# Scores and turned scores of one image in four PSUM banks, with maximum and exponential in two halves each: an audio encoder block on one Trainium2 core

## The reference

```python
# 1. time-delay layer with batch norm: windows of 5 frames, 115 values
y = relu(patches @ W.T + b)                       # (32, 121, 128)
h = (y - mean(y)) * rsqrt(var(y) + 1e-5) * gamma + beta
# 2. attention, per image, 8 heads of 16, bias per key column and head
z = layernorm(h)
scores = q(z) @ k(z).T / 4 + col_bias             # (32, 8, 121, 121)
h = h + o_proj(softmax(scores) @ v(z))
# 3. top-1 mixture of 8 experts, 128 -> 512 -> 128
z = layernorm(h)
e, gate = argmax(z @ Wr + br), 1                  # a softmax over one value is 1
h = h + relu(z @ W1[e] + b1[e]) @ W2[e] + b2[e]
```

## Time and profile before

| | us |
|---|---|
| median of three runs | 311.4 (311.34 to 316.01) |
| the profiled execution | 310.43 |
| its span in the trace | 308.7 |
| attention loop, maximum of image 0 to the last turned maximum | 45.3 to 199.0 |
| first matmul of the expert stage's first tile | 224.6 |

### The profile page before, as it was taken

One profiled execution on the slowest core, in us unless ns is written; L12 is line 12 of the kernel. 1 busy time (PEld: TensorE's weight loads), 2 busy tenths in 40 slices (PEclk: granted clock), 3 DMA queues, 4 the chain that ended last, 5 costly groups with the idle time before them and its releaser, 6 DMA issues.

```text
span 308.7 us, 9094 instructions
## 1 busy us (share of the span) xinstructions
PE 263.8 (85%) x2915; PEld 223.6 (72%) x2915; DVE 187.5 (61%) x690; ACT 165.3 (54%) x395; POOL 141.8 (46%) x256
## 2 busy tenths in 40 slices
PE   3898479999999999999999999883099999999960
PEld 2767357778778777877778786562099999999960
DVE  3887233476777768677686777746436556555540
ACT  3861122566655666466664654521067777777730
POOL 7000640343438646476565654347215555555560
PEclk9995575999999999999999999955579999999996
DMA  3200399100001101010010110111243334334200
GB/s 104 71 2 0 98 345 317 47 3 2 2 3 35 32 18 35 19 37 25 28 32 19 34 35 18 35 52 49 74 115 86 101 87 120 98 93 122 79 7 0
DMA packets 15374, 19.14 MB, mean 62 GB/s; under 512 B 4007, under 2 KB 11467, under 8 KB 15328
## 3 DMA queue, kind: packets, MB, share of 16 engines
q1 hardware_dynamic: 11888, 12.15, 14.0%
q0 software_dynamic: 3296, 6.00, 6.6%
q10 hardware_dynamic: 144, 0.41, 0.4%
HBM read 10.58 MB, written 8.47 MB: 62 GB/s over the span
## 4 chain that ended last, share of the span: by engine, by line
PE 71%; issue 9%; POOL 7%; DVE 5%; ACT 3%; DMA 2%; SPq 1%; POOLq 0%; DVEq 0%
PE psS L1089 11%; PE psS L921 10%; PE psB L904 9%; PE psO L1052 5%; PE psO L1100 5%; PE psU L1100 5%; PE psU L1001 4%; PE psU L1005 4%; PE psB L893 3%; POOL region_d L376 3%; PE psB L910 2%; DVE nmax L750 2%; ACT patT L421 2%; PE psU L1044 2%; PE psS L928 2%
## 5 line engine op out<-in xcount | busy, mean ns | idle before, releaser
L404 POOL DMA_INDIRECT out<-y_out,sidx x38 | 36.9, 971 | 45.6 <-DVE y_out L824 41.2
L495 ACT ACTIVATE PT<-psS 121x968 f32<-121x968 f32 x32 | 31.3, 977 | 37.7 <-PE psS L928 37.7
L921 PE MATMUL psS<-kT,qT 32*121 32x121 f32 x512 | 45.7, 294 | 4.9 <-ACT xT L448 2.0
L376 POOL DMA_INDIRECT region_d<-rows,pos x32 | 34.7, 1085 | 31.2 <-DVE pos L709 21.2
L928 PE MATMUL psS<-qm,kT 32*121 32x121 f32 x512 | 45.7, 295 | 0.0
L833 DVE TENSOR_SCALAR hT<-psS,b1T 128x128 f32<-128x128 f32 x76 | 23.3, 347 | 34.9 <-PE psS L1089 34.8
L921 PEld LDWEIGHTS psS<-kT,qT 32*121 32x121 f32 x512 | 34.1, 185 | 13.7 <-issue 9.3
L1089 PE MATMUL psS<-xgT,W_tile 128*128 128x128 f32 x304 | 41.7, 282 | 0.0
L750 DVE TENSOR_REDUCE nmax<-psS 121x8 f32<-121x968 f32 x32 | 37.0, 1157 | 5.6 <-PE psS L921 5.5
L1089 PEld LDWEIGHTS psS<-xgT,W_tile 128*128 128x128 f32 x304 | 38.5, 199 | 0.0
L928 PEld LDWEIGHTS psS<-qm,kT 32*121 32x121 f32 x512 | 33.6, 185 | 0.4 <-DVE qm L765 0.3
(11 more groups left out here) (222 smaller groups left out, 578.4 us busy)
## 6 DMA issues: line engine op xcount, KB each, us to landing
xg<-region_d SPq DMA_DIRECT2D x38, 129.0 KB, 2.1
W_sb<-in_L_ffn_W SPq DMA_DIRECT2D x1, 2048.0 KB, 9.9
region_d<-pads SPq DMA_DIRECT2D x1, 1032.0 KB, 6.9
region_d<-pads SPq DMA_DIRECT2D x1, 903.0 KB, 8.8
out<-y_out,sidx POOLq DMA_INDIRECT x38, 2.8
b_bc<-in_L_ffn_b SPq DMA_DIRECT2D x1, 512.0 KB, 5.1
region_d<-rows,pos POOLq DMA_INDIRECT x32, 3.0
xs<-in_x ACTq DMA_DIRECT2D x1, 402.5 KB, 3.6
```

The lines of the kernel that those rows point to most:

```text
L376: pool.indirect_dma_start(region_d, bass.IndirectOffsetOnAxis(pos[0:L, b:b + 1], 0), rows[0:L, b, E:E + ROW], None, bounds_check=E * CAP - ...
L404: pool.indirect_dma_start(out, bass.IndirectOffsetOnAxis(sidx[:, s:s + 1], 0), y_out[:, u, :], None, bounds_check=N - 1, oob_is_err=False) ...
L495: act.activation(PT[0:L, (t - 1) % 2, :, :, :], score_set(t - 1), ACT.Exp).then_inc(s_exp, 1)
L921: ins = pe.matmul(psJ[0:L, t % 2 * HG + j, a * 128:a * 128 + L], qT[rws, t // 2 % 2, a, n0:n0 + L], kT[rws, t // 2 % 2, a, n0:n0 + L], sta ...
```

## The change

It rearranges the attention loop. Scores of image t take the first half of the columns of all four banks, the turned scores of image t - 1 the second half. `scores` and `scores_T` are now one block each, without the wait for the first half (`s_half`). DVE takes the maximum of banks 0 and 1, then that of banks 2 and 3; ACT takes the exponential of banks 2 and 3, then that of banks 0 and 1; each waits for the other before it crosses over. What follows the product with V comes one step later than before for each image (`has(t, 3)` to `has(t, 5)` in place of 2 to 4), the denominators are turned back with two whole transposes, `on` is scaled in two instructions, and the ranks move from `psU` to the second bank of `psB`. The order within each engine's step is new. `h0_copy(p + 3)` stands at the end of the even step, `squares1(p + 2)` near the end of DVE's even step. POOL's order is as it was, but for `rstd2`, of image t - 4 now. The bodies of `h0_copy`, `norm1_first`, `norm1_second`, `squares1`, `k_copy`, `q_copy` and the expert functions are unchanged.

```diff
-            return b0 + nb + 4
+            return b0 + nb + 5
...
-        psJ = psS[:, :, :].rearrange("p b (h n) -> p (b h) n", n=256)
-        def score_set(t):
-            return psJ[0:L, t % 2 * HG:t % 2 * HG + HG, :].rearrange("p j (a n) -> p j a n", a=2)[:, :, :, 0:L]
+        def score_half(turned, pair):
+            return psS[0:L, 2 * pair:2 * pair + 2, turned * 256:turned * 256 + 256].rearrange("p j (a n) -> p j a n", a=2)[:, :, :, 0:L]
...
@@ POOL
-                if has(t, 3):
-                    rstd2(t - 3)
+                if has(t, 4):
+                    rstd2(t - 4)
...
@@ ACT
             for t in range(STEPS):
                 p, even = t // 2, t % 2 == 0
-                if has(t, 2):
-                    act.wait_ge(s_PV, t - 1)
-                    act.activation(OTs[:, :, :], ...
-                if not even and p + 3 < NP:
-                    h0_copy(p + 3, psB[:, 1, :])
+                if not even and p + 1 < NP:
+                    q_copy(p + 1, psB[:, 0, :])
                 if even and p > 0 and p + 3 < NP:
                     batch_norm(p + 3)
-                if has(t, 4):
-                    b = t - 4
+                if has(t, 5):
+                    b = t - 5
                     act.wait_ge(s_r2, b + 1)
                     act.activation(rows[0:L, b, WX:WX + D], rows[0:L, b, E:E + D], ACT.Identity,
                                    scale=rs2[0:L, b % 4:b % 4 + 1]).then_inc(s_x2, 1)
                 if has(t, 1):
                     act.wait_ge(s_ST, t)
+                    if has(t, 0):
+                        act.wait_ge(s_S, t + 1)
                     if t >= 3:
                         act.wait_ge(s_PV, t - 2)
-                    act.activation(PT[0:L, (t - 1) % 2, :, :, :], score_set(t - 1), ACT.Exp).then_inc(s_exp, 1)
+                    act.activation(PT[0:L, (t - 1) % 2, 2:4, :, :], score_half(1, 1), ACT.Exp).then_inc(s_exp, 1)
+                if has(t, 4):
+                    act.wait_ge(s_OT, t - 3)
+                    act.activation(oT[:, :], psO[:, 256:256 + L], ACT.Identity).then_inc(s_oT, 1)
+                if has(t, 1):
+                    if has(t, 0):
+                        act.wait_ge(s_max, 2 * t + 1)
+                    act.activation(PT[0:L, (t - 1) % 2, 0:2, :, :], score_half(1, 0), ACT.Exp).then_inc(s_exp, 1)
+                if even and p < NP:
+                    v_copy(p, psB[:, 0, :])
                 if has(t, 2):
+                    act.wait_ge(s_PV, t - 1)
+                    act.activation(OTs[:, :, :], ...
+                if even and p + 3 < NP:
+                    h0_copy(p + 3, psB[:, 1, :])
                 if not even and p + 2 < NP:
                     xT_copy(p + 2, psB[:, 1, :])
...
@@ DVE
-                if not even and p + 1 < NP:
-                    k_copy(p + 1)
-                if even and p >= 1 and p + 2 < NP:
-                    squares1(p + 2)
...
+                if has(t, 0):
+                    dve.wait_ge(s_S, t + 1)
+                    if t > 0:
+                        dve.wait_ge(s_ST, t)
+                    for pair in range(2):
+                        if pair == 1 and t > 0:
+                            dve.wait_ge(s_exp, 2 * t - 1)
+                        dve.tensor_reduce(..., score_half(0, pair), AX.X, ALU.max, negate=True).then_inc(s_max, 1)
+                for g in range(NG):
+                    if ranked(g) == t:
+                        row_places(g)
+                if has(t, 5):
+                    ... (lg of image t - 5)
+                if has(t, 0):
+                    dve.wait_ge(s_nT, t + 1)
+                    dve.tensor_tensor(qm[:, :, :], ...
+                if not even and p + 1 < NP:
+                    k_copy(p + 1)
+                if has(t, 4):
+                    dve.wait_ge(s_P, t - 3)
                 if has(t, 3):
+                    ... (rden, then on in two instructions)
+                if has(t, 4):
+                    ... (rows, then sq2, of image t - 4)
+                if even and p >= 1 and p + 2 < NP:
+                    squares1(p + 2)
+                for g in range(NG):
+                    if ranked(g) - 1 == t:
+                        expert_max(g)
+                        expert_rank(g)
+                        expert_onehot(g)
+                        expert_seen(g)
...
@@ PE, the order of a step after; waits in brackets
+ scores(t)        [exponential of t - 2, maximum of t - 1; even: k_copy and q_copy of the pair]
+ scores_T(t - 1)  [qm of t - 1]
+ turn on(t - 4)   [on; OTs(t - 3)]
+ turn back t - 3  [rows of t - 5; OTs(t - 3)], two transposes into psU
+ even: values(p), transpose_h0(p + 3); odd: k projection of p + 1 [q_copy of p + 1]
+ output projection of t - 4 [oT]
+ rank_rows if due (odd steps)
+ turn nmax(t)     [both maxima], the mark
+ product with V of t - 2
+ even: q projection of p + 1 [v_copy]; odd: transpose_xn(p + 2)
```

More of the change, by code:

```diff
@@ L988, in _ @@
                         pe.wait_ge(s_qs, 2 * p + 2)
+                    scores(t)
                 if has(t, 1):
                     pe.wait_ge(s_qm, t)
-                if t <= B:
-                    scores(t, 0)
-                if has(t, 3):
-                    if t >= 4:
-                        pe.wait_ge(s_h1, t - 3)
-                    for g in range(NG):
-                        if ranked(g) + 2 == t:
-                            pe.wait_ge(r_pick, g + 1)
-                    pe.wait_ge(s_oT, t - 2)
-                    pe.matmul(psU[0:L, 128:128 + WX], oT[:, :], owX[:, :], start=True, stop=True).then_inc(s_P, 1)
-                if has(t, 2):
-                    pe.wait_ge(s_OTs, t - 1)
+                    scores_T(t - 1)
+                if has(t, 4):
+                    pe.wait_ge(s_on, t - 3)
+                    if has(t, 3):
+                        pe.wait_ge(s_OTs, t - 2)
+                    pe.transpose(psO[:, 256:256 + L], on[0:L, :], ident[0:L, 0:L]).then_inc(s_OT, 1)
+                if has(t, 5):
+                    pe.wait_ge(s_h1, t - 4)
+                if has(t, 3):
+                    pe.wait_ge(s_OTs, t - 2)
                     for a in range(2):
-                        ins = pe.matmul(psU[0:L, 272 + a * HG * (HD + 1):272 + (a + 1) * HG * (HD + 1)], OTs[:, a, :],
-                                        ident[:, :].rearrange("p (j c) -> p j c", c=HB)[:, :, 0:HD + 1], start=True, stop=True)
+                        ins = pe.transpose(psU[0:L, 258 + a * 113:258 + a * 113 + 128], OTs[:, a, :], ident[:, :])
                     ins.then_inc(s_bT, 1)
-                if t <= B:
-                    pe.wait_ge(s_half, t + 1)
-                    scores(t, 1)
-                if even and p + 1 < NP:
+                if even and p < NP:
+                    values(p, psB[:, 0, :])
+                if even and p + 3 < NP:
                     if p > 0:
-                        pe.wait_ge(s_qs, 2 * p + 2)
+                        pe.wait_ge(s_xT, p + 2)
+                    transpose_h0(p + 3, psB[:, 1, :])
+                if not even and p + 1 < NP:
+                    pe.wait_ge(s_qs, 2 * p + 4)
                     for g in range(2):
@@ L1017, in _ @@
                     ins.then_inc(s_k, 1)
-                if not even and p + 1 < NP:
-                    pe.wait_ge(s_kT, p + 2)
+                if has(t, 4):
+                    pe.wait_ge(s_oT, t - 3)
+                    pe.matmul(psU[0:L, 121:121 + WX], oT[:, :], owX[:, :], start=True, stop=True).then_inc(s_P, 1)
+                for g in range(NG):
+                    if ranked(g) == t:
+                        pe.wait_ge(s_h0k, min(p + 4, NP))
+                        if g > 0:
+                            pe.wait_ge(r_pick, g)
+                        rank_rows(g)
+                if has(t, 0):
+                    pe.wait_ge(s_max, 2 * t + 2)
+                    pe.transpose(psU[:, 0:L], nmax[0:L, :], ident[0:L, 0:L]).then_inc(s_nT, 1)
+                if has(t, 2):
+                    pe.wait_ge(s_exp, 2 * t - 2)
+                    pe.wait_ge(s_Vs, (t - 2) // 2 + 1)
+                    if has(t, 4):
+                        pe.wait_ge(s_oT, t - 3)
+                    for a in range(2):
+                        for j in range(HG):
+                            ins = pe.matmul(psO[j * HB:(j + 1) * HB, a * 128:a * 128 + L], V[0:L, (t - 2) // 2 % 2, t % 2, a * HG + j, :],
+                                            PT[0:L, t % 2, j, a, :], start=True, stop=True)
+                    ins.then_inc(s_PV, 1)
+                if even and p + 1 < NP:
+                    pe.wait_ge(s_Vs, p + 1)
                     for g in range(2):
```

144 lines of the change are left out of this document (45 added, 99 removed).

## The result

| | before | after |
|---|---|---|
| median | 313.7 us (4 runs, 311.3 to 316.8) | 393.2 us (4 runs, 391.0 to 396.7) |
| ratio after / before | | 1.261, 95% interval 1.246 to 1.275 |
| profiled execution / its span | 310.43 / 308.7 | 396.65 / 394.8 |
| marks of steps 2 to 26 | 117.3 | 193.7 |
| marks of steps 26 to 31 | 23.3 | 28.3 |

What follows compares the result with a forecast made beforehand. PE's stream bounds the kernel before; after, a loop over DVE, POOL and ACT: 2.4 + 5.4 + 2.7 + 5.1 = 15.6 us a pair. 308.7 + 1.7 + 66.1 + 5.1 - 1.5 + 0.5 = 380.6, + 17 for the clock = 397; range 366 to 427.

Steps and rivals of the forecast that it cites:

- squares1 to h0_copy, 5.4: Loop term on POOL: from DVE's squares1 to the start of ACT's h0_copy, 5.4 us with a scatter.
- Even mark to the end of squares1, 2.4: Loop term on DVE: from the even step's turned maximum (its mark) through qm to the end of squares1, 2.4 us.
- h0_copy to the odd mark, 2.7, at low clock 4.0: Loop term on ACT, with PE beside it: h0_copy to the odd step's mark, 2.7 us; half clock adds 1.35.
- Odd mark to even mark, 5.1: Loop term: ACT's way through x2, exponential and second maximum, 5.1 us, longer than PE's way of 4.4.
- Mark 2 to 26, 183.4 at full clock and 17 for the clock, 200.4 in all: Twelve pairs of the loop: 179.9 us plus some 0.7 for each of five odd steps, then 17 for the clock.
- The start, -1.5: Ahead of mark 2: step 0's scores on four strips and k projection leaving that step save 1.5 us (0 to -2.5).
- The end, +0.5: After the last mark: chain one step deeper, but POOL's scatters set the end, +0.5 us (-1 to +2).
- The clock: PE idle from the odd step's scores to q_copy's end: clock falls each pair, part of each burst slow, +17 us.
- 425 of the low clock throughout: Rival: same loop with PE at low clock throughout, 15.6 + 3.7 us a pair, 425 us; chance 0.2.
- 381 without a fall: Rival: PE's clock does not fall in the loop's idle, 381 us; chance 0.15.
- rival in which only `x2` is the gate, 355: ACT's x2 in the odd step, not the copy, waits for POOL's root: 13.3 us a pair, 355 us; chance 0.05.
- rival with PE's stream, 304: POOL's bias write lands early, neither copy nor x2 delays ACT's exponential, PE's stream sets the pace: 304 us; chance 0.03.

Runs made afterwards that it cites:

- e3: Changed kernel with matmuls whose result nobody reads put into PE's idle of the odd steps, ahead of the k projection; 379.1 us, 1.212 to the kernel before.
- e8: Changed kernel with x2 behind both exponentials on ACT, nothing else; 385.4 us, 1.236 to the kernel before.
- e1: Changed kernel with squares1(p + 2) back at the start of DVE's even step, ahead of the first maximum; 343.8 us.
- e2: Changed kernel with two h0k buffers, so h0_copy(p + 3) waits for norm1_second(p + 1), no order changed; 366.2 us, 1.169 to the kernel before.
- e6: Changed kernel with two h0k buffers, squares1 first, rstd2 ahead of POOL's scatters, x2 behind both exponentials; 299.6 us, 0.960 to the kernel before.
- e7: Changed kernel, one h0k buffer, squares1 first, norm1_second directly behind norm1_first, x2 behind both exponentials; 300.5 us, 0.961 to the kernel before.
- e4: Kernel before with only squares1(p + 2) moved to the end of DVE's even step, behind qm; 381.8 us, 1.217 to the kernel before.
- e11: e6 with the two score blocks apart, the turned scores behind the two groups of transposes; 318.3 us, 1.027 to the kernel before.
- e10: e6 with denominators turned back by the old two float32 matmuls and `on` in one instruction; 302.6 us, 0.975 to the kernel before.

## Why the prediction was right

The mechanism is the one foreseen: the ring over DVE, POOL and ACT closes once a pair, at the foreseen places, and PE's clock falls in its gap. That the total comes within 4 us is partly luck: the loop was put some 7 us too long and the end 6 us too short.

- *squares1 to h0_copy, 5.4:* squares1's reading of the sum ends at 150.43, the copy starts at 155.81: 5.38. Without a scatter and with it, `h0k` waits 4.6 and 6.3 us in the trace.
- *Even mark to the end of squares1, 2.4:* 148.25 to 150.43, 2.2. The copy, foreseen at 7.8 after the mark, came at 7.6.
- *h0_copy to the odd mark, 2.7, at low clock 4.0:* 3.4 (159.19 less 155.81) in a pair without ranks, 4.2 with them; 2.6 and 2.9 in e3, at full clock. So the low clock costs 0.8 and 1.3 here, where I had 1.35.
- *Halves, 0.65 and 0.58:* 0.66 for the maximum, 0.58 for the exponential.
- *Odd mark to even mark, 5.1:* 5.05 to the marks of steps 8, 12, 16, 20 and 24; 6.2 to 6.5 to those of 10, 14, 18 and 22, where the clock was low (5.25 in e3).
- *Mark 2 to 26, 183.4 at full clock and 17 for the clock, 200.4 in all:* 193.7. e3 measures the clock's part at 17.9 and the rest at 175.9. The 7.5 too much are mostly in the pairs up to step 10, 51.5 us in e3 against some 56, and more than half of these in the first pair: in step 2 DVE has no `rden`, `on` or `sq2` yet, so squares1 ended 1.2 us after the mark (57.77 less 56.58) and not 2.4, and `x2` does not yet exist in step 4, so its gate could not cost there (4.2 in place of 5.1).
- *Marks 26 to 31, 28.5:* 28.3, though the clock there was 0.88.
- *The start, -1.5:* -1.9. But between the profiled executions of the changed kernel's variants the mark of step 2 stands anywhere from 53.5 to 56.6, so this agreement says little.
- *The end, +0.5:* **this term failed.** It measured +6.5. I had put it that the scatters of POOL set the end, as many as before. But the root of image 31 ends 19.3 us after the last mark, before at 12.4; the timelines of POOL of before, after and e8 (last marks at 199.03, 278.64 and 270.64):

```profile
210.84 0.57 POOL L370 TENSOR_TENSOR rs<-var,minus_half 121x1 f32<-121x1 f32 x1
```

```profile
297.37 0.57 POOL L368 TENSOR_TENSOR rs<-var,minus_half 121x1 f32<-121x1 f32 x1
```

```profile
286.28 0.57 POOL L368 TENSOR_TENSOR rs<-var,minus_half 121x1 f32<-121x1 f32 x1
```

  In the last steps hardly an exponential or a projection is left to hide anything, and an image needs one step more than before. Each of these steps holds two waits for POOL's root of the image whose `sq2` ended the step before: `lg` on DVE, and `x2` on ACT, behind which `oT` and `OTs` stand. e8 shows what the second is worth: with `x2` behind both exponentials the root comes at 16.2 and the end at 112.5 after the last mark, 3.7 us earlier than in the change (e1, e2 and e3, which leave `x2` where it is, have 115.8 to 116.2). The other 2.8 us I put down to the one step more and `lg`; that was not tested apart. The error is 6 us, of the other sign to that in the loop.
- *The clock:* it fell in each of the twelve pairs. In the 1 us windows of one pair (early and late in PE's idle, and after PE has resumed; the clock third from last):

```profile
153.00:154.00 1.00, 0.00 (x0) 0.00 (x0) 0.00 (x0) 0.00 (x0) 0.94 (x2) 1.00 0.00 0
...
155.00:156.00 1.00, 0.00 (x0) 0.00 (x0) 0.00 (x0) 0.19 (x1) 0.79 (x2) 0.50 0.03 9
...
162.00:163.00 1.00, 1.00 (x23) 0.89 (x16) 0.50 (x1) 0.42 (x3) 0.57 (x1) 1.00 0.00 0
```

  The rule of the Trainium skill ("TensorE: Matmul & The Clock Gate", section "HAM oscillation — how this bites in real kernels") and this trace agree in ten of the twelve pairs, whose bursts began at 1.2 GHz; in the first two, after gaps of 1.8 and 3.6 us, the burst began at 2.4 GHz and the clock fell 0.7 and 1.2 us into it. The 425 of the low clock throughout and the 381 without a fall are both refuted; e3 shows that 381 would have been right had the clock stayed up (379), with the same two errors in it. The price of 17 was right in sum (17.9) but not in its parts: I had the low clock for the front of each burst, and in every second pair it lasted some 9 us, through the scores of the even step.
- *The range, 366 to 427:* it holds the three clock cases with 15 us below the lowest and 2 above the highest, and not with 10 below, as I had written.
- *The rival in which only `x2` is the gate, 355:* not what the change does, but e2 makes it so and gives 366; its wait is there (54.4 us), its clock was left out.
- *The rival with PE's stream, 304:* e6 and e7 open its gate and give 300. PE's saving was mis-sized: 0.75 a pair by my terms, of which 0.35 was left after the even step's wait for k_copy; from 117.3 to 106.7 it is 0.89 a pair, net of that wait.

What stays open: what the halves and their crossing cost by themselves was not tried; e6 only shows that with the new order of PE they cost less than it brings. The end stays open too: e6 and e7 still take 114.6 and 113.1 us from the last mark, where the kernel before took 109.7.

## What to carry to other kernels

Moving a small instruction within one engine's step moves the whole chain that begins at it: before placing it, follow that chain through the other engines to the next wait in an in-order queue, and ask what stands behind that wait. A wait that is nearly harmless (6.8 us in seven places, all of it covered) is the one to look at first, because it says how little slack is left. And when a repair is sought, opening the first gate shows the second at once (e2 after `h0k`, e4 before `lg`); list them all first, then open them together.

## What the runs showed of the hardware

- In the kernel after, the granted clock fell from 2.4 to 1.2 GHz in each of twelve pairs, 2.4 to 4.8 us after PE had stopped. In the last eight pairs PE stood idle for 5.2 to 5.6 us and the fall came 2.8 to 4.0 us into the gap, so the low level was paid by the work after the gap, not by the gap. There it came back 4.2 to 4.6 us after PE resumed in some pairs (156.9 to 161.4) and 8.5 to 9.0 us in others (173.0 to 181.9), in turn. Matmuls put in for nothing (e3) paid for themselves: 17.9 us of 193.7.
- A passage of PE from blocks on 32-row strips to full-array matmuls costs about 0.19 us in the first full-array instruction, and the way back about 0.21 (e6 against e11), at full clock. The Trainium skill ("TensorEngine Tiling (Array Packing)", Key Properties) says that a change of the tiling mode drains TensorE, without a price. The trace agrees in that each passage costs time, some 0.2 us each way here; the drain itself is not to be seen in it. Keeping the two score blocks together was worth more here (0.4 us a step, and 0.60 with what followed from it, e11) than the cheaper transposes (0.11 us a step, e10).
